# The result layer with samples as loaded weights, and results stored a sample to a partition

## The reference

```python
combined = jnp.concatenate([dense_features[:, None, :], sparse_features], axis=1)      # 2048 x 27 x 128
interactions = jnp.einsum('bnd,bmd->bnm', combined, combined)
z = jnp.concatenate([dense_features, interactions[:, _TRIU_I, _TRIU_J]], axis=1)
h = jnp.concatenate([z, r_dense_features], axis=1)                                      # 2048 x 607
h = jnp.maximum(h @ W_top1 + b_top1, 0.0)                                               # 512 columns
h = jnp.maximum(h @ W_top2 + b_top2, 0.0)                                               # 256 columns
y = h @ W_top3                                                                          # 1 column
```

## Time and profile before

| | us |
|---|---|
| time, median of three runs | 371.13 |
| the three runs | 369.68 to 371.79 |
| the profiled execution's own time | 370.95 |
| its span | 369.1 |
| TensorE matmul busy | 337.2 (91%) |
| weight loads busy (beside matmuls) | 312.4 (85%) |
| VectorE, ScalarE busy | 206.5, 205.0 (56% each) |
| GpSimd busy | 258.4 (70%) |

### The profile page before, as it was taken

One profiled execution on the slowest core, in us unless ns is written; L12 is line 12 of the kernel. 1 busy time (PEld: TensorE's weight loads), 2 busy tenths in 40 slices (PEclk: granted clock), 3 DMA queues, 4 the chain that ended last, 5 costly groups with the idle time before them and its releaser, 6 DMA issues.

```text
span 369.1 us, 9446 instructions
## 1 busy us (share of the span) xinstructions
PE 337.2 (91%) x4000; PEld 312.4 (85%) x4000; DVE 206.5 (56%) x379; ACT 205.0 (56%) x253; POOL 258.4 (70%) x280
## 2 busy tenths in 40 slices
PE   0486879999999999999999999998999979999986
PEld 0486779998999889998999889996999859998785
DVE  4799745982099406980199406980099402960140
ACT  2698474547644656457544655456644655456412
POOL 6777777777777777777777777777777777777100
PEclk9998998999999999999999999999999999999999
DMA  6999524872256214742267224741256212622330
GB/s 172 250 252 197 177 71 149 227 233 55 55 125 222 70 50 98 190 129 59 54 128 224 63 58 97 214 107 52 54 128 218 72 52 62 148 62 60 73 41 19
DMA packets 49316, 43.98 MB, mean 119 GB/s; under 512 B 33359, under 2 KB 39094, under 8 KB 49274
## 3 DMA queue, kind: packets, MB, share of 16 engines
q1 hardware_dynamic: 39166, 25.36, 27.3%
q0 software_dynamic: 8704, 17.84, 18.5%
q10 hardware_dynamic: 1404, 0.17, 0.3%
HBM read 37.91 MB, written 5.44 MB: 117 GB/s over the span
## 4 chain that ended last, share of the span: by engine, by line
PE 51%; POOL 24%; DMA 9%; issue 9%; ACT 3%; SPq 2%; ACTq 1%; DVE 0%
POOL rows L407 24%; PE banks L457 23%; PE banks L478 10%; DMA hidden<-in_tbl_dram 6%; PE mlp L499 6%; PE moved L432 5%; PE mlp L509 5%; DMA rows<-in_tbl_dram,ids_sb 2%; SPq L256 2%; ACT products L875 1%; ACT vectors L862 1%; ACTq L234 1%; DMA scratch<-products 1%; DMA features<-scratch 1%; PE mlp L520 1%
## 5 line engine op out<-in xcount | busy, mean ns | idle before, releaser
L407 POOL DMA_INDIRECT rows<-in_tbl_dram,ids_sb x272 | 257.5, 947 | 83.9 <-issue 80.2
L701 DVE TENSOR_TENSOR masks<-hot_ids,row_of 125x512 fp32r<-125x512 int32 (+1 forms) x336 | 182.3, 621 | 97.8 <-PE banks L457 92.4
L457 PE MATMUL banks<-masks,high 125*128 125x256 f32 x592 | 150.7, 294 | 16.1 <-DVE low L688 16.1
L457 PE MATMUL banks<-masks,low 125*128 125x256 f32 x592 | 146.8, 287 | 0.0
L457 PEld LDWEIGHTS banks<-masks,high 125*128 125x128 f32 x592 | 115.8, 196 | 16.9 <-issue 14.6
L457 PEld LDWEIGHTS banks<-masks,low 125*128 125x128 f32 x592 | 115.9, 196 | 0.0
L845 ACT ACTIVATE vectors<-banks 128x512 f32<-128x512 f32 (+1 forms) x40 | 40.4, 1010 | 79.9 <-PE banks L457 79.9
L862 ACT ACTIVATE vectors<-moved 128x512 f32<-128x512 f32 (+1 forms) x79 | 78.1, 988 | 6.5 <-PE moved L432 6.5
L478 PEld LDWEIGHTS banks<-vectors 128*64 128x64 f32 x2048 | 63.2, 141 | 8.3 <-issue 7.6
L875 ACT ACTIVATE products<-banks 123x432 f32<-123x432 f32 x62 | 57.8, 947 | 18.3 <-PE banks L478 15.7
L478 PE MATMUL banks<-vectors 128*64 128x54 f32 x2048 | 66.3, 226 | 0.8 <-ACT vectors L862 0.5
(11 more groups left out here) (50 smaller groups left out, 67.3 us busy)
## 6 DMA issues: line engine op xcount, KB each, us to landing
hot_ids<-in_ids_of_field_dram SPq DMA_DIRECT2D x32, 256.0 KB, 4.7
rows<-in_tbl_dram,ids_sb POOLq DMA_INDIRECT x272
features<-scratch SPq DMA_DIRECT2D x7, 351.0 KB
scratch<-products SPq DMA_DIRECT2D x56, 42.2 KB
scratch<-products SPq DMA_DIRECT2D x28, 81.2 KB
w_sb<-in_tbl_dram SPq DMA_DIRECT2D x3, 448.0 KB
hot_ids<-in_ids_of_field_dram SPq DMA_DIRECT2D x8, 128.0 KB
dense_sb<-in_dense_dram SPq DMA_DIRECT2D x8, 128.0 KB, 5.5
```

The costliest lines, as they stand in the source:

```text
L407: pool.indirect_dma_start(rows[:, (tile * TILE_ROWS + v) % RING, :], None, tables[f][:, :], bass.IndirectOffsetOnAxis(ap=ids_sb[:, tile, f ...
L457: last = nc.tensor.matmul(banks[:, j % BANKS, m * CHUNK:(m + 1) * CHUNK], part[:, part_of(j * PAIR + m, k), :], masks[:, mask % MASK_RING, ...
L701: nc.vector.tensor_tensor(masks[:, mask % MASK_RING, 0:size], hot_ids[0:PART_ROWS, n % ID_RING, 0:size], row_of[0:PART_ROWS, row:row + 1]. ...
```

## The change

The result layer turns its operands round. `last_layer(c)` loads 128 samples of one half as weights (128 hidden units by 128 samples) and moves one column of `w3`; the two blocks of hidden units add up in one column of `mlp`, so that the chunk's results are two columns on 128 partitions, a sample to a partition. All four matmuls form one group, and the wait for the second of the two kept blocks stands ahead of the first. So that a half is 128 neighbouring columns, the second layer's writes (L902, L735) put the samples into their order: four bytes are written every 16. `keep_y` copies two columns into a new tile `results` with two buffers, and `store_y` sends each column as 128 pieces of four bytes. The waits for `out_written` stay where they are. Chunk 7's second layer and result layer stay as they are.

```diff
+        results = sb("results", [128, 2, HALVES])
...
                 for half in range(HALVES):
                     first = c * CHUNK + half * HALF
-                    sp.dma_start(out[first:first + HALF, :].rearrange("b o -> o b"),
-                                 hidden2[half * STRIP:half * STRIP + 1, 1, 0:HALF]).then_inc(out_written, 16)
+                    sp.dma_start(out[first:first + HALF, :],
+                                 results[:, c % 2, half:half + 1]).then_inc(out_written, 16)
...
-                for m in range(MTILES2):
-                    pe.wait_ge(second_kept, MTILES2 * c + m + 1)
-                    for half in range(HALVES):
-                        to = half * STRIP
-                        last = nc.tensor.matmul(mlp[to:to + 1, 0, 0:HALF], w3_sb[:, m:m + 1],
-                                                hidden2[:, m, :].rearrange("d (q g) -> d q g", q=QUADS)[:, :, groups_of(half)],
-                                                start=(m == 0), stop=(m == MTILES2 - 1),
-                                                tile_position=(0, to))
+                pe.wait_ge(second_kept, MTILES2 * (c + 1))
+                for half in range(HALVES):
+                    for m in range(MTILES2):
+                        last = nc.tensor.matmul(mlp[:, 0, half:half + 1],
+                                                hidden2[:, m, samples_of(half)],
+                                                w3_sb[:, m:m + 1],
+                                                start=(half == 0 and m == 0), stop=(half == HALVES - 1 and m == MTILES2 - 1))
                 last.then_inc(y_ready, 1)
...
-                nc.vector.tensor_scalar(hidden2[:, 1, :], mlp[:, 1, 0:CHUNK], b2_sb[:, 1:2], 0.0,
+                nc.vector.tensor_scalar(hidden2[:, 1, :].rearrange("p (g q) -> p q g", q=QUADS),
+                                        mlp[:, 1, 0:CHUNK].rearrange("p (q g) -> p q g", q=QUADS), b2_sb[:, 1:2], 0.0,
                                         ALU.add, ALU.max).then_inc(second_kept, 1)
...
-                nc.vector.tensor_copy(
-                    hidden2[0:Y_ROWS, 1, 0:HALF].rearrange("o (g q) -> o q g", q=QUADS),
-                    mlp[0:Y_ROWS, 0, 0:HALF].rearrange("o (q g) -> o q g", q=QUADS)).then_inc(y_kept, 1)
+                nc.vector.tensor_copy(results[:, (LAST - 1) % 2, :], mlp[:, 0, 0:HALVES]).then_inc(y_kept, 1)
...
-                nc.scalar.activation(hidden2[:, m, :], mlp[:, m, 0:CHUNK], ACT.Relu, bias=b2_sb[:, m:m + 1])\
+                nc.scalar.activation(hidden2[:, m, :].rearrange("p (g q) -> p q g", q=QUADS),
+                                     mlp[:, m, 0:CHUNK].rearrange("p (q g) -> p q g", q=QUADS),
+                                     ACT.Relu, bias=b2_sb[:, m:m + 1])\
                     .then_inc(second_kept, 1)
...
-                nc.scalar.activation(
-                    hidden2[0:Y_ROWS, 1, 0:HALF].rearrange("o (g q) -> o q g", q=QUADS),
-                    mlp[0:Y_ROWS, 0, 0:HALF].rearrange("o (q g) -> o q g", q=QUADS), ACT.Copy).then_inc(y_kept, 1)
+                nc.scalar.activation(results[:, c % 2, :], mlp[:, 0, 0:HALVES], ACT.Copy).then_inc(y_kept, 1)
```

## The result

The changed kernel takes 381.95 us (median of four runs, 378.62 to 383.49) against 371.46 us for the kernel before beside it (369.68 to 371.82): a ratio of 1.027, 95% interval 1.023 to 1.031, some 10.5 us slower. The prediction was 371.4 us and no change that could be told; it was wrong.

What follows compares the result with a forecast made beforehand. GpSimd's gathers were taken to bound the kernel until 302.34 us, TensorE's chain after; 0.21 us (layer) plus 0.1 (stores) gave +0.3 on 371.13, so 371.4 us, no visible change, range 370.1 to 372.8.

Steps and rivals of the forecast that it cites:

- the stores: Result stores on SP's queue: 256 more packets, 16 an engine at 12.6 ns; between 0 and 0.2 us, taken as +0.1.
- The sign named for this: Tail: last load issued or landing over 0.5 us later, counted from the last scratch write, would show the stores misjudged.
- The cover named for the stores: Tail, SP's queue: 1.1 us between the pair's issue ending and half 1's feature load at 358.70 absorb the small packets.
- The small stores hold up the tail: Rival: chunk-6 stores delay half 1's features and VectorE's write of half 0; 374.3 us at 0.25 us a packet; chance 0.07.
- 16p - 1.1: Tail: us the end moves if each of 16 packets an engine costs p us, beyond 1.1 us of cover.
- The price taken, 0.25: Tail stores: assumed us per 4-byte packet in the slower rival, moving the end by 2.9 us to 374.3.
- the layer: Result layer on TensorE: eight loads 0.112 us apart take 0.90 us for 0.69, +0.21 us a call, one call on path.
- the range of the distance named: TensorE between two look-ups: 1.16 to about 1.37 us expected; under 1.0 or over 1.9 would show the layer wrong.
- load and matmul don't overlap: Rival, TensorE's result layer: each pass takes the whole 192 ns, +0.85 on the path and 0.5 in tail, 372.6 us; chance 0.1.
- GpSimd paces the loop: Loop: 272 gathers at L407, one every 1.25 us, held up by nothing; TensorE waits for them until 302.34.
- covers the early calls: Chunks 0 to 4: TensorE's idle 0.94 and 2.76 us hide five result-layer calls, otherwise 1.05 us.
- the strided write of the second layer: ScalarE, L902: every fourth word written, 0 to 0.14 us longer each, two hidden by 0.61 us idle before keep_step.

Runs made afterwards that it cites:

- e9: Changed kernel with chunks 0 to 5 stored as 512-byte rows, only chunk 6's tail stores left as 4-byte pieces: 379.76 us, ratio 1.023.
- e3: Changed kernel with its 4-byte pieces sent to a scratch tensor in HBM, 512 bytes apart: 371.12 us, ratio 1.000.
- e5: Changed kernel with its 4-byte pieces sent to a scratch tensor in HBM, 64 bytes apart: 371.45 us, ratio 0.999.
- e8: Changed kernel with its 4-byte pieces sent to a scratch tensor in HBM, 32 bytes apart: 372.53 us, ratio 0.999.
- e6: Changed kernel with its 4-byte pieces sent side by side to a scratch tensor in HBM instead of the output: 380.85 us, ratio 1.023.
- e2: Changed kernel with its small stores alone undone, halves leaving as 512-byte rows: 370.66 us, ratio 0.998.
- e10: Changed kernel with chunk 6's tail stores as 512-byte rows, the loop's stores (chunks 0 to 5) left as 4-byte pieces: 370.95 us, ratio 1.001.
- e1: Kernel before with only the stores of chunks 0 to 6 made 128 side-by-side 4-byte pieces each: 379.18 us, ratio 1.022.
- e4: Changed kernel with even and odd samples in two columns, one store of 128 8-byte pieces a chunk: 373.13 us, ratio 1.005.

## Why the prediction was wrong

- **The failed step is the term "the stores".** It took 16 packets an engine at 12.6 ns, 0.2 us of which +0.1 was counted, from 128-byte packets. Its row was the wrong kind twice over: it has the length of packets, while the price of these pieces stands in no packet of their own (9 ns each), and the pieces of that row begin no closer than 128 bytes to each other. Measured in its place: 9.0 us from issue to release for the pair, 8.85 us on the time (e9). The sign named for this, the last load issued or landing over 0.5 us later, came.
- **The cover named for the stores failed with it.** The 1.1 us between the pair's issue and the load at 358.70 was to hide 16 packets an engine. The pair also held up a write issued ahead of it, the last scratch write (6.22 us in place of 2.65), on which the load waits; the prediction looked only at what stands behind the stores.
- **The right rival had a chance of 0.07.** "The small stores hold up the tail" named the place, the two waits (the load, VectorE's write of half 0) and the form, 16p - 1.1. At the measured 9.0 / 16 = 0.56 us a packet it gives 7.9 us, and 8.85 came; that it comes so near is partly luck, since the form holds neither the late scratch write (3.6 us) nor the clock (1.6). The price taken, 0.25, was less than half of that. It fell short in weight because the small packets of the earlier trace rows spoke against it, and in the range, which stopped at 372.8 with this rival's own 374.3 outside. The Trainium skill's page "DMA: Bandwidth & Descriptors" (section Specifications) was cited there for read-modify-write below 512 bytes. If that rule alone made the price, e3, e5 and e8 would pay like e6, and they pay nothing. The Trainium skill's page "Collectives: The Full Stack" (section "Rules for kernel authors") asks for buffers aligned to 32 bytes, so that no read-modify-write arises. The step between 8 and 32 bytes agrees with that figure, if pieces that share 32 bytes are rewritten one after another. That this is the mechanism was not shown.
- **Missed altogether**: the clock. Behind 5.80 us without work TensorE came back to a granted clock of 0.50 until 375.20; L544's twelve matmuls took 2.90 us for 1.58, and 1.6 us of the loss are this.
- **Right**: the layer, +0.16 us a call for +0.21 forecast, with loads 0.113 us apart for 0.112; the range of the distance named, 1.0 to 1.9 us, holds 1.32. With it falls the rival "load and matmul don't overlap". The rule of the Trainium skill's page "TensorE: Matmul & The Clock Gate" (section "Part 3: Packing small matmuls") that the prediction cited disagrees with these 0.113 us. **Right**: that GpSimd paces the loop (1.25 us) and covers the early calls; e2, the whole change with harmless stores, whose chain still waits for a gather issued at 298.88, is at 0.998, where the forecast was +0.3 us. In the changed kernel's own profile that cover is gone behind 158.87, with TensorE on the chain from there.
- **Mis-sized without harm**: the strided write of the second layer, bounded at +0.14 us from a row of 614 ns and measured at 724 - 473 = +0.25; two of them come to 0.50 and still fit the 0.61 us of the earlier trace rows, of which 0.36 are left in the changed kernel.

## What to carry to other kernels

A store that scatters a column over partitions is to be priced by how close its pieces lie in memory: side by side, 256 pieces of 4 bytes held a tail up for 9 us, while the same pieces 32 bytes apart, or one row, cost no time that showed. Such a price doesn't show in the packets that cause it; look for it in other queues' packets and in what lands late around the store, ahead of it as well as behind. And a long wait in the chain is worth its length only if nothing later would have waited anyway: a gather of 11.59 us to land cost e10 nothing in the loop, while a store of 9 us to land in the tail cost e9 nearly all of it.

## What the runs showed of the hardware

- Stores of pieces that lie side by side in device memory are slow: 256 pieces of 4 bytes took 7.9 to 9.1 us from issue to release (changed kernel, e1, e6, e9), 128 of 8 bytes 4.3 us (e4). At 32, 64 and 512 bytes apart the 256 pieces landed in 2.0 to 2.1 us (e8, e5, e3).
- While they drain, transfers of other queues wait: gather packets took up to 7.4 us for 1.3 before, and a write whose packets had ended at 361.37 had its last completion at 365.45, with the DMA engines recorded 3% busy.
- Eight full-array loads with a one-column matmul each take 0.98 us, 0.113 us apart, the same as loads ahead of 128-column matmuls (0.112, from the earlier trace rows).
- ScalarE's write of every fourth word costs 724 ns for 256 columns, 473 for words in a row, 614 for words 128 bytes apart.
- Behind 5.8 us of idle TensorE in the tail the granted clock was 0.82 on average, 0.50 at first and 1.00 later, while in e10, without that idle time, it was 1.00 (the last stretch shown, columns as above):

```profile
360.20:368.10 7.90, 5.52 (x47) 4.82 (x44) 0.73 (x2) 2.22 (x6) 0.00 (x0) 1.00 0.01 2
```
